# Cross attention and a top-2 expert layer on one core: the expert stage is run in two phases, 41 tiles first and 30 after the last batch is routed

## The reference

```
x = x + attention(layernorm(x), ctx)          # 16 heads of width 16, softmax over 512 keys
z = layernorm(x)
probs = softmax((z @ Wg + bg) / 5.0)          # 8 experts
gates = the two largest probs, divided by their sum, zero elsewhere
x = x + sum_e gates[e] * (gelu(z @ W1[e] + b1[e]) @ W2[e] + b2[e])   # hidden width 512
```

## Time and profile before

| | |
|---|---|
| runs | 869.04, 860.61, 870.62 us; median 869.04 |
| the profiled execution | 858.64 us, span of its trace 856.8 us, mean granted clock 0.937 |
| TensorE busy | 766.0 us, 89% of the span |
| VectorE busy | 630.3 us, 74% |
| ScalarE busy | 452.4 us, 53% |
| GpSimd busy | 370.7 us, 43% |
| DMA | 122.60 MB, mean 143 GB/s |

### The profile page before, as it was taken

The page is one execution under the profiler, slowest core; times in us unless marked ns, Lnnn a source line. Parts: engine busy times, 40 slices in busy tenths (PEclk is TensorE's granted clock), DMA queues, the critical chain, the costliest instruction groups (busy, mean ns, idle before and its releaser), DMA issues. The chain is left out here.

```text
span 856.8 us, 16256 instructions
## 1 busy us (share of the span) xinstructions
PE 766.0 (89%) x4697; PEld 460.4 (54%) x4697; DVE 630.3 (74%) x1113; ACT 452.4 (53%) x669; POOL 370.7 (43%) x342
## 2 busy tenths in 40 slices
PE   8599899999999999999999787331999999999995
PEld 4243344444444444444444332120899999999995
DVE  6786777797797797897787875365677777777774
ACT  3066775766766767766666555220444444444442
POOL 6406153266276176176244052304244444444444
PEclk9589999999999999999999988655999999999998
DMA  6857575676675676567367332244244444444441
GB/s 216 206 152 212 134 202 180 172 227 198 173 244 167 175 244 181 149 229 202 109 219 213 90 110 69 89 196 134 46 80 77 79 81 74 78 75 78 77 75 13
DMA packets 89083, 122.60 MB, mean 143 GB/s; under 512 B 15032, under 2 KB 51864, under 8 KB 88744
## 3 DMA queue, kind: packets, MB, share of 16 engines
q1 hardware_dynamic: 74632, 103.69, 42.2%
q0 software_dynamic: 13296, 17.09, 11.2%
q10 hardware_dynamic: 1072, 0.79, 0.3%
HBM read 64.44 MB, written 57.22 MB: 142 GB/s over the span
## 5 line engine op out<-in xcount | busy, mean ns | idle before, releaser
L860 DVE TENSOR_REDUCE negm<-ring 128x2 f32<-128x1024 f32 x256 | 310.3, 1222 | 76.9 <-PE ring L1233 74.7
L784 ACT ACTIVATE probs<-ring 128x1024 f32<-128x1024 f32 x256 | 260.7, 1024 | 98.0 <-PE ring L1246 97.6
L706 POOL DMA_INDIRECT out<-y_sb,xs x71 | 110.6, 1557 | 150.5 <-DMA out<-y_sb,xs 81.9
L1259 PE MATMUL ps_pv<-probs,v_aug 128*32 128x512 f32 x1024 | 138.6, 613 | 5.3 <-ACT probs L784 5.2
L1246 PE MATMUL ring<-q_st,k_st 64*128 64x512 f32 x512 | 128.0, 499 | 4.6 <-DVE negm L860 4.5
L1233 PE MATMUL ring<-k_st,q_st 64*128 64x512 f32 x512 | 110.4, 432 | 12.7 <-ACT probs L784 5.7
L1246 PEld LDWEIGHTS ring<-q_st,k_st 64*128 64x128 f32 x512 | 48.3, 186 | 105.8 <-issue 76.4
L612 POOL DMA_INDIRECT xs_dram<-xg,rows x64 | 65.4, 1021 | 81.0 <-DVEq L1023 51.1
L1404 PE MATMUL ring<-w_hi,hT_hi 128*128 x284 | 85.7, 302 | 0.1
L1404 PE MATMUL ring<-w_lo,hT_hi 128*128 x284 | 80.4, 283 | 0.0
L1404 PE MATMUL ring<-w_hi,hT_lo 128*128 x284 | 79.7, 281 | 0.0
(11 more groups left out here) (167 smaller groups left out, 1240.5 us busy)
## 6 DMA issues: line engine op xcount, KB each, us to landing
k_st<-k_dram SPq DMA_DIRECT2D x64, 192.0 KB
q_st<-q_dram SPq DMA_DIRECT2D x64, 192.0 KB
xs<-xs_dram SPq DMA_DIRECT2D x71, 132.5 KB, 2.3
k_dram<-qk_hi SPq DMA_DIRECT2D x32, 256.0 KB
q_dram<-qk_hi SPq DMA_DIRECT2D x32, 256.0 KB, 2.9
o_dram<-oT SPq DMA_DIRECT2D x32, 256.0 KB, 3.9
x_all<-in_x SPq DMA_DIRECT2D x8, 512.0 KB, 4.9
k_dram<-qk_lo SPq DMA_DIRECT2D x16, 256.0 KB
```

What stands on the lines that cost most here:

```text
L706: pool.indirect_dma_start(out=out, out_offset=bass.IndirectOffsetOnAxis(ap=xs[:, j % AHEAD, TOKEN:TOKEN + 1].bitcast(I32), axis=0), in_=y_ ...
L784: nc.scalar.activation(probs[:, kt, 2 * jp:2 * jp + 2, :], ring[PLACE["ST", u, p] % RINGS][:], ACT.Exp).then_inc(exp_done, 1)
L860: nc.vector.tensor_reduce(negm[:, v % 2, :, jp, kt], ring[PLACE["MX", v, p] % RINGS][:], AX.X, ALU.max, negate=True).then_inc(max_free, 1)
L1259: mm = nc.tensor.matmul(ps_pv[2 * DH * j:2 * DH * (j + 1), :], v_aug[:, kt, HPG * g + j, :], probs[:, kt, j, :], start=(kt == 0), stop=(kt ...
```

## The change

The tiles are split in two runs. Six batches have 6144 pairs; each expert may leave up to 127 rows over, so at least `TILES1` = 41 tiles are full after six batches whatever the routing. These are taken from the counts of batches 0 to 5 (`CN` is now run twice, at `(1, 2)` of batch 7 and at tile 26), their tables are made on VectorE in group 2 of batch 7 (`first_tables`), and the stage starts when batch 7's attention ends. The other `TILES2` = 30 start behind the rows taken, expert 0 to 7 once more (`last_tables`). What batch 7 still needs is put behind tiles of the first run:

```
+TAIL_PE = {6: "OP0", 7: "OP1", 8: "OP2", 9: "OP3", 17: "XG0", 18: "XG1", 19: "LG", 25: "PX", 26: "CN"}
+TAIL_LN2 = {10: "stats0", 11: "stats1", 12: "sums"}
+TAIL_ROUTE = {21: "softmax", 22: "first", 23: "second", 24: "gates"}
+TAIL_TABLES = {27: "tiles", 28: "past", 29: "rows"}
+TAIL_NORMALISE, TAIL_APPLY, TAIL_EXP, TAIL_POW, TAIL_SCATTER = 5, (15, 16), 20, 13, 25
+TAIL_STORE, TAIL_PAD = 18, 36
```

The weights are split elsewhere. GpSimd in batch 7 (the order is its program order), and after its body:

```
             def body(i):
...
+                if i == B - 1:
+                    for e in range(E):
+                        high_w1(e)
                 if i > 1:
                     scatter(i - 2, NP * (NG * i + 1) + SCATTER if i < B - 1 else None)
+                if i == B - 1:
+                    for e in range(2):
+                        low_w1(e)
                 if i > 0:
                     ln2(i - 1)
+                if i == B - 1:
+                    for e in range(2, E - 2):
+                        low_w1(e)
...
                 if i == B - 1:
                     scatter(i - 1)
...
-            ln2(B - 1)
-            scatter(B - 1)
-            pool.wait_ge(out_done, 16 * B)
+            low_w2(1, 1)
+            low_w2(5, 2)
             token_bound = pool.to_reg(TOKENS - 1)
+            pool.wait_ge(out_done, 16 * (B - 1))
             pool.wait_ge(need_done, 1)
...
             for j in range(TILES):
+                if j == TAIL_POW:
+                    ln2(B - 1)
+                if j == TAIL_SCATTER:
+                    rows_ready(B - 1)
+                if TAIL_SCATTER <= j < TAIL_SCATTER + TOPK * NT:
+                    scatter_tile(*divmod(j - TAIL_SCATTER, NT))
+                if j == TILES1:
+                    pool.wait_ge(out_done, 16 * B)
+                    pool.wait_ge(need_done, 2)
                 add_out(j)
```

ScalarE makes `w2_hi` of experts 0 and 4 in group 1 and of 3 and 7 after `high_xt(0)`; it waits for the first tables before it copies `XG0` of batch 6, since these tables lie in `xgT`. VectorE's places in batch 7, and what it does between batch and tiles:

```
+LAST_COUNT = {(1, 2): "CN"}
+LAST_TABLES = {(2, 0): "tiles", (2, 2): "past", (2, 4): "rows"}
+LAST_LOW_W1 = {(2, 1): 6, (2, 3): 7}
+LAST_HIGH_W2 = {(2, 5): 1, (2, 6): 5, (3, 7): 2}
+LAST_LOW_W2 = {(2, 7): 0, (3, 0): 4}
+LAST_HIGH_W2_ACT = {(1, 2): 0, (1, 5): 4}
...
+            high_w2(6)
...
             low_xt(0)
+            low_w2(2, w2_hi_dve, 3)
+            low_w2(6, w2_hi_dve, 4)
+            reciprocals(B - 1, 1)
             low_xt(1)
+            low_w2(3, w2_hi_act, 3)
+            low_w2(7, w2_hi_act, 4)
+            dve.wait_ge(tab_done, 1)
             e = {0: expert_of(0), 1: expert_of(1)}
+            dve.wait_ge(b1_in, 32)
+            dve.wait_ge(b2_in, 16)
             take_h(0, e[0])
             for j in range(TILES):
                 if j + 1 < TILES:
                     take_h(j + 1, e[j + 1])
                 if j + 2 < TILES:
+                    if j + 2 == TILES1:
+                        dve.wait_ge(tab_done, 2)
                     e[j + 2] = expert_of(j + 2)
                     low_xt(j + 2)
                 low_ht(j)
                 if j > 0:
                     take_y(j - 1, e.pop(j - 1))
+                tail(j)
```

TensorE uses one bank for `turn_x`, and waits for the second weights only before the first `output`:

```
             def turn_x(j):
                 pe.wait_ge(xs_in[j % AHEAD], 16 * (j // AHEAD + 1))
-                if j >= 2:
-                    pe.wait_ge(f_xt_out, j - 1)
+                if j > 0:
+                    pe.wait_ge(f_xt_out, j)
+                else:
+                    pe.wait_ge(o_out, G)
...
+            pe.wait_ge(tab_done, 1)
+            e = {0: expert_of(0), 1: expert_of(1)}
             turn_x(0)
+            pe.wait_ge(w1_split, E)
+            hidden(0, e[0])
             turn_x(1)
...
                 turn_h(j)
                 if j > 0:
+                    if j == 1:
+                        pe.wait_ge(w2_split, E)
                     output(j - 1, e.pop(j - 1))
+                if j in TAIL_PE:
+                    misc(TAIL_PE[j], 1 if TAIL_PE[j] == "CN" else B - 1)
```

SyncE after its body loads the rows of tiles 0 to 3, then `b1` in two halves (each after one `pv` step of the last group; `b2` now goes in batch 7), stores `o` of the last group, loads tiles 4 to 7, and only then issues `put_recip` and `fetch_o` of batch 7:

```
+            sp.wait_ge(tab_done, 1)
+            sp.wait_ge(scattered, 16 * TOPK * NT * EARLY_B)
+            for j in range(EARLY_XS + 1):
+                load_rows(j)
+            for n in range(2):
+                load_b1(n)
             put_o(G - 1)
+            for j in range(EARLY_XS + 1, AHEAD):
+                load_rows(j)
             put_recip(B - 1, 1)
             fetch_o(B - 1, 1)
+            bring_x(B - 1)
+            for j in range(AHEAD, TILES):
+                if j == TAIL_STORE:
+                    store_out(B - 1)
+                if j == TAIL_PAD:
+                    pad_regions()
+                if j == TILES1:
+                    sp.wait_ge(tab_done, 2)
+                    sp.wait_ge(dummy_in, 16)
+                    sp.wait_ge(scattered, 16 * TOPK * NT * B)
+                    sp.wait_ge(padded, 16 * E)
                 load_rows(j)
```

More of the change, by code:

```diff
@@ L112, in units @@
     last = i == B - 1
+    if last and (g, p) in LAST_COUNT:
+        out.append((LAST_COUNT[g, p], 0))
     for table, b in (((LAST_LATE if last else LATE), i - 2), ((LAST_POST if last else POST), i - 1),
@@ L283, in build, with end, table @@
         y_sb = sb("y_sb", [P, RING, D])
+        xs = [sb(f"xs{k}", [P, ROW_W]) for k in range(EARLY_XS)]
+        with ExitStack() as attention_end:
+            def end(name, shape, dt=F32):
+                return attention_end.enter_context(nc.sbuf_tensor(name, shape, dt))
+            mT = end("mT", [HPG * NT, 2, P], F32R)
+            bq_sb = end("bq_sb", [P, DC])
+            bk_sb = end("bk_sb", [P, DC])
+            stats = end("stats", [P, NT, 6])
+            oT = end("oT", [P, 2, S])
+        xs += [sb(f"xs{k}", [P, ROW_W]) for k in range(EARLY_XS, AHEAD)]
+        numT = sb("numT", [P, DC, S])
+        recT = sb("recT", [P, S])
+        den = sb("den", [P, DC, 2 * DH])
+        with ExitStack() as tables:
+            def table(name, shape, dt=F32):
+                return tables.enter_context(nc.sbuf_tensor(name, shape, dt))
+            past = table("past", [P, TILES1, E])
+            past_n = table("past_n", [P, TILES1, E])
+            first_of = table("first_of", [P, TILES1])
+            need_up = table("need_up", [P, TILES, RING], I32)
+            need_sh = table("need_sh", [P, TILES, RING], I32)
+        xgT = sb("xgT", [P, DC, S])
+        wo_sb = sb("wo_sb", [P, DC, D])
+        e_of = sb("e_of", [P, TILES1])
+        start_of = sb("start_of", [P, TILES2])
+        live = sb("live", [P, TILES2])
+        e_tab = sb("e_tab", [P, TILES], I32)
+        row_tab = sb("row_tab", [P, TILES], I32)
+        need = sb("need", [P, TILES, RING], I32)
         ring = [stack.enter_context(nc.psum_tensor(f"ring{n}", [P, 2, S], F32)) for n in range(RINGS)]
@@ L794, in body @@
                             route_exp(i - 1)
+                        if i == B - 1 and (g, p) in LAST_HIGH_W2_ACT:
+                            high_w2(LAST_HIGH_W2_ACT[g, p])
             for name in PROLOGUE:
@@ L841, in _ @@
             high_xt(0)
+            high_w2(3)
+            high_w2(7)
             high_xt(1)
@@ L902, in misc @@
                     route_rows(b)
+                elif name == "CN":
+                    dve.wait_ge(full["CN"], b + 1)
+                    nc.vector.tensor_copy(counts[:], ps_x[:, 0:E]).then_inc(done["CN"], 1)
                 elif name[:2] == "OP":
@@ new lines, in low_w2, with added_before @@
+            def low_w2(e, high, count):
+                dve.wait_ge(high, count)
+                nc.vector.tensor_tensor(w2_lo[:, e], x_all[:, e * NT:(e + 1) * NT, :], w2_hi[:, e].bitcast(F32),
+                                        ALU.subtract).then_inc(w2_split, 1)
+            def added_before(lo, n):
+                v, k = nc.vector, (RING + 1) * (lo > 0)
+                for r in range(RING):
+                    v.tensor_scalar(need_up[:, lo:lo + n, r], first_of[:, 0:n], float(lo + RING - 1 - r), None, ALU.add).then_inc(need_chain, 1)
+                dve.wait_ge(need_chain, k + RING)
+                v.tensor_scalar(need_sh[:, lo:lo + n, :], need_up[:, lo:lo + n, :], RING.bit_length() - 1, None,
+                                ALU.arith_shift_right).then_inc(need_chain, 1)
+                dve.wait_ge(need_chain, k + RING + 1)
+                v.tensor_scalar(need[:, lo:lo + n, :], need_sh[:, lo:lo + n, :], 1.0, 16.0, ALU.max, ALU.mult).then_inc(need_done, 1)
@@ L1054, in body @@
                     for p in range(NP):
-                        if last and g >= 2:
-                            e, low = divmod(NP * (g - 2) + p, 2)
-                            if low:
-                                low_w1(e)
-                            else:
-                                high_w1(e)
                         for v, q in ahead(u, p):
@@ L1111, in _ @@
-            for e in range(E // 2):
-                low_w2(e)
-            route_logits(B - 1)
-            for part in ROUTE.values():
-                route(part, B - 1)
-            route_rows(B - 1)
-            v = nc.vector
-            dve.wait_ge(full["CN"], 1)
-            c = Chain(dve, tab_chain, 15, 0)
-            c.link(v.tensor_copy(counts[:], ps_x[:, 0:E]))
```

(2 more changed lines are left out.)

382 lines of the change are left out of this document (235 added, 147 removed).

## The result

The changed kernel takes **828.36 us** (median of four runs, 827.25 to 835.44) and the kernel before 867.36 us in four runs on the same chip: a ratio of **0.9619 (0.9565 to 0.9674)**. The medians lie 39 us apart, which alone would be 0.955; the ratio, the more cautious of the two, makes it 33 us, and ratios are used from here on. 828 was predicted, with 814 to 849 as the range. The profiled execution took 829.04 us, its span 827.3 against 856.8.

The account below looks back on a forecast made before the run. Expert stage bound by TensorE, with 68.5 us of mostly small batch 7 steps between attention and first `output`. 556.3 + 250.7 + 8 + 2 + 4 = 821 span; 823 with 1.84 around it, plus 5: 828 us, range 814 to 849.

Parts of the forecast that it names:

- rival 2: Nothing collides: VectorE never held, attention 2.5 us early, tail's VectorE work hidden; 819, with the lower offset 816; chance 0.16.
- the signs by which the prediction would be wrong: Attention of batch 7 ending after 548, or TensorE waiting in the second run.
- The attention's end: End of batch 7's last attention product, forecast to move from 537.64 to 539.1, bounds 533.6 to 547.4.
- (a): Batch 7's attention: without VectorE's w1 splits beside GpSimd's `ln2`, xg is ready earlier; 2.5 us gained, bounds 0 and 4.
- rival 3: GpSimd's reads hold VectorE throughout: 9.8 us instead of 4 in group 0, more later; 843; chance 0.16.
- (b): Batch 7's attention: GpSimd's eight w1 casts beside batch 5's routing hold VectorE's small steps; +4 us, at worst 9.8.
- GpSimd's line: From attention to first `output`: 1.5 us, scatter of batch 6 10.5, two `low_w2` 5.2; comes last, at 556.3.
- The other line: From attention to first `output`, o's copy through VectorE's `low_w2` and GELU: about 11 us, near 550, 6 before GpSimd's.
- Behind the first `output`: Added to the 250.7 us: TensorE's work of batch 7 +8, clock +2, VectorE's tables and row numbers +4.
- The +2 of the clock: After TensorE's 6 us wait for `low_w2`, some 4 us at half rate behind 556; +2 us, 0 to 4.
- rival 5: Slower: the single bank of `turn_x` puts transpose, cast and difference in every tile's path; 927; chance 0.03.
- rival 4: Second run: adds that begin an expert wait for the landing of the one before; gain given back, 858; chance 0.05.

Follow-up runs that it names:

- 12: The changed kernel once more, unaltered, on the chip of 9 and 10: 833.09 us, ratio 0.9657 to the kernel before.
- 5: Changed kernel with the second run's tables at tiles 28, 31 and 34 in place of 27, 28 and 29: 831.35 us, 0.9633.
- 2: Changed kernel with GpSimd's four differences of w1 in group 2 waiting until the first tables are done: 829.88 us, 0.9635.
- 6: Changed kernel with all eight w1 differences on VectorE, none on GpSimd, which keeps the casts: 825.04 us, 0.9565.
- 8: Changed kernel with each of GpSimd's six w1 differences replaced by two fills, leaving out low parts of experts 0 to 5: 827.03 us, 0.9592.
- experiment 7: Changed kernel with GpSimd's eight w1 casts replaced by zero fills that read nothing, leaving out w1's high parts: 827.82 us in one execution.
- 9: Changed kernel with 6 and 4 together, and `take_h(0)` on VectorE ahead of `low_w2` of experts 3 and 7: 830.87 us, 0.9633.
- 10: 9 with the second run's tables cut into six pieces, behind tiles 27, 28, 30, 31, 33 and 34: 828.59 us, 0.9616.
- 13: 6 with the six table pieces of 10, against the changed kernel: 826.41 us, 0.9573.
- 1: Changed kernel with the first tables made one group earlier, in group 1 of batch 7 instead of group 2: 835.62 us, 0.9715.
- 3: Changed kernel with GpSimd's eight w1 casts waiting until VectorE has made its choice for batch 5: 830.29 us, 0.963.
- 4: Changed kernel with `low_w2` of experts 1 and 5 on GpSimd ahead of the scatter of batch 6: 830.05 us, 0.9621.

## Why the prediction was right, and where it was not

The way the time is saved came out as forecast: the first `output` is 44.5 us earlier (I had 49.8), and 15.0 us are added behind it (I had 14). That the median is 828 to the microsecond is luck, two errors that cancel. My span was 821 and the changed kernel's is 827.3: 6 us too low. I added 5 for the place of the median above the profiled execution, and here the median lies 0.7 below it. (The low end of my range is written as 814 and called rival 2 with the lower offset, which is 816 a few lines above. Nothing hangs on it.)

Of the signs by which the prediction would be wrong, one came: TensorE waits in the second run, 1.4 us in this execution and nothing in 12. The attention's end stayed below 548 here, but not in 12 (554.2) nor in 5 (548.5), which has the same code up to there.

- **(a) The wait for `xg`, -2.5: wrong.** The half that I read from the rows was right: TensorE waits 1.67 us for `xg` where it was 3.97. The step that failed is "about 8 us behind the layer norm's sums, so about when xg is ready". I priced the chain of the tables by rows in which GpSimd stood still, though I had GpSimd's differences at 2.56 each on the same page and the collision as rival 3, and never laid the four of them beside the chain. They held three steps for 6.2 us more than these take alone. TensorE's 5.30 for the copy, less the 2.3 gained, makes +3.0 in place of -2.5. Experiments 2, 6 and 8 each take the hold away in another manner and all find the copy's wait at 1.57 to 2.95. The hold and the wait are shown. That they are worth 3.0 us of the attention's end is not: in 6 and 8 the wait is gone, and `XG0` to the end still takes 24.1 and 24.2 us, at a low clock.
- **(b) The casts beside the routing, +4: right in size.** 3.3 of direct hold. `numT`, the numerators of batch 6, come 4.7 us later (497.3 for 492.6) and `veps`, the variance of the second layer norm, 3.7 (512.8 for 509.1). A cast took 0.99 us, not 1.22. In experiment 7, with nothing read, `veps` comes 0.9 us later than before, so 2.8 of the 3.7 went with the reading. It is one execution, and what of the 2.8 is the hold and what the clock behind it stays open.
- **The attention's end**, 539.1 predicted, bounds 533.6 to 547.4: 545.4, inside and near the top, as rival 3 would have it. After `XG0` it took 24.9 us instead of 18.5: 5.3 of it is the wait for the copy, the rest the half clock, more of it than before. I had no clock term there.
- **GpSimd's line.** The scatter began at 544.41, 1.0 us before the attention's end and not 1.5 behind it. It took 12.3 us, not 10.5; `low_w2` 4.72, not 5.2. So the first `output` came 16.1 us after the attention and not 17.2: at 561.6 for 556.3.
- **The other line** came second, as said, but TensorE was idle for 2.44 us ahead of the first `output` and not 6.
- **Behind the first `output`**, +14 predicted, +15.0 measured. TensorE's work of batch 7: 8.6 by the groups, taken as 8; `PX` and `CN` are 1.5 and not 0.7. VectorE's row numbers and tables: 3.4 for the 4. The second run: 2.2, of which TensorE waits 1.4, which I had at nothing. These make 14.2; in the rest is the clock between 670 and 680, at 0.80 and 0.86. The +2 of the clock behind the first `output` did not come: from 560 to 670 it is at 1.00.
- **At nothing and found so:** ScalarE's change of table at tile 20 (the tiles there keep 3.46 and 3.47 us), the single bank of `turn_x` (rival 5: no tile shows a wait for it, and tiles 35 to 54 keep 3.46), SyncE's empty rows.
- **At nothing and found otherwise: rival 4.** Its mechanism is there. The add of a tile waits for the landing of others, the buffers of `y_sb` come free late, and VectorE and then TensorE wait: the sign that I had named, a tile pitch other than 3.47 in tiles 42 to 66. It costs 2.2 us and not 30, since most tiles make it up. In the seven traces looked at (changed, 5, 6, 9, 10, 12, 13) every wait of VectorE for a landing of 1.6 us or more in the second run reached TensorE, and none under 1.5 did; in 12, the same kernel again, the longest was 1.41 and TensorE waited for nothing there. No experiment takes these waits away.
- **Rivals.** The mechanism of rival 3 is real, and in group 2 it acts as rival 3 has it. It did not decide, since in group 0 the five held products cost 3.3 us where rival 3 had 9.8. Rival 2 is excluded by the same rows.

Where the expected extra gain went, when I took these holds away one at a time, is what experiments 1 to 4 show: each moved the collision to another instruction of VectorE that stands beside GpSimd's, and only those that take the reading off GpSimd (6 and 13, and 7 and 8, which leave work out) kept a part.

## What to carry to other kernels

When work is moved to an idle GpSimd, lay its instructions beside VectorE's in time: a chain of n small steps there can be held n times, once by each long instruction, and a 2.3 us difference turned three steps of 0.2 us into 6.8. If VectorE does the same work in half the time, it is better left there. A tail of one batch can be put under tiles of another stage at little more than its bare cost of instructions; a piece longer than the slack of one tile makes TensorE wait wherever it stands. In a stretch with gaps a change of 2 or 3 us drowns in where the clock falls, so judge it from one event to the next and by the clock beside it, and run the same code more than once to see how far apart two executions lie.
